# Four-layer attention and feed-forward stack on one core: first stacks over two DMA queues, three PSUM banks each for maxima and scores, values of two key tiles every four steps

## The chip, the cores and the metric

One core of one Trainium2 chip runs the whole program. The metric is the device time of one launch in microseconds. A compute engine is called PE (TensorE), DVE (VectorE), ACT (ScalarE) or POOL (GpSimd); SP is the sync engine, which here only issues DMAs.

## The reference, cut to what matters

Eight sequences of 512 rows and 256 features go through four layers. Each layer is an attention and a feed-forward part with residuals. The change touches the one program stage that computes three of these parts: the cross attention of layer 0, its "ffn" (an attention with gates), and the cross attention of layer 1.

```
q, k, v = heads(x @ Wq.T + bq), heads(ctx @ Wk.T + bk), heads(ctx @ Wv.T + bv)   # 16 heads of 16
attn = softmax(q @ k.T / sqrt(16));  out = (attn @ v) @ Wo.T + bo;  x = x + out
# gated part: q from the row's own norm, direction and temperature; k and v from x itself;
# head output times a gate from softmax(h @ Wr), softmax(h @ Ws) and the top 3
```

## The kernel before, in words

The stage is `softmax_attentions`. It works through 24 items (8 sequences of layer 0's cross attention, kind "cross"; 8 of the gated one, kind "mixture"; 8 of layer 1's cross attention), and each item has 32 steps. Every engine runs the same nest, item by item and step by step (`rounds`), from two rounds ahead of the first item (numbers -2 and -1) to one behind the last. Nothing schedules at run time: the order of each engine's instructions is what its `steps` function writes, and tables of (step, what, half) put the side work.

One step of one item does two of the 64 score tiles and two of the 64 tiles for maxima:

- **M**, `for_maximum` (L745): queries times keys into one bank of `ps_max`, 128 queries by 512 keys; DVE reduces the bank to a row maximum (`maximum`, L479). It runs `LEAD` = 12 steps ahead of the scores. There are 2 banks, so M number u waits for the reduction of M number u-2.
- **S**, `score` (L734): keys times queries, with the negated maxima as extra rows of the stacked operand, into `ps_sc`. ACT takes the exponential (`exponentials`, L661). There are 4 banks, used as two pairs: one step's two S fill a pair, and one ACTIVATE of 1024 columns empties it into `probs`, which has 4 slots (of one step each).
- **V**, `values` (L756): at every odd step, four heads' probabilities of one key tile times `vpad` (16 value columns and a column of ones, 32 columns per head), on four column tiles of PE at once, summed in `ps_out` over four key tiles. PE shows 8 matmuls for it. Every 8 steps ACT copies `ps_out` out (`take_out`, L669, step 2 of 8), and the first V of the next group of heads waits for that copy.
- **Fills** share one bank, `ps_t`, and each waits until the one before has been taken: projections "k" and "q" (L768), "v" and "y" (L776, 8 matmuls), transposes "xnT", "hT" (L763) and "raw" (L814), and "negmax" (L808), which turns the negated maxima. ACT then writes them beside the queries (`take_negmax`, L674), DVE takes v (L495), raw (L504, L506) and y (L583, or L587 in mixture items). The table `TURNS` says at which step each is made: in a cross item, for instance, v at steps 9 and 10, hT at 11 and 12, negmax at 5, 13, 21, 29.

The order of S and M on PE is S M S M at odd steps and M S S M at even ones, then V at odd steps.

Operands are stacked: the three bf16 parts of queries and keys go to a scratch in HBM (L304) and come back as 12 DMAs of 256 KB per item, 16 partitions each (`stacked`, L299), 6 for `kstack` and 6 for `qstack`. The first M of an item waits for all 12 (`stack_in`). For the first item, in the lead-in, SP issues the 6 of keys, the 6 of queries, then the second item's context (`kv_in`, L286), then six sequences of x. PE's order puts the second item's two "k" fills, which read that context, before the first M.

## Time and profile before

| what | value |
|---|---|
| median of 3 runs | 4552.01 us (4549.38 to 4552.75) |
| the profiled execution, its own time | 4549.59 us |
| its span, first to last instruction | 4547.6 us |
| PE busy, share of the span | 4283.4 us, 94% |
| DVE busy | 2994.0 us, 66% |
| ACT busy | 2515.0 us, 55% |

The span is what the profile divides; 2.0 us lie around it. Busy PE means that a matmul is under way: its end is modelled, and matmuls overlap, so 94% doesn't mean that PE could not take more. A line such as L745 is a line of the kernel before; in the changed one the numbers are some ten to twenty higher.

### The profile page before, as it was taken

The page shows a single profiled execution, that of the slowest core. Times are in us where ns is not written, and L with a number is a line of the kernel's source. Part 1 is how long each engine was busy: PE and PEld are TensorE (multiplying, and loading weights), DVE is VectorE, ACT ScalarE, POOL GpSimd, SP SyncE. Part 2 cuts the span into 40 slices and gives each one's busy share as a digit, 9 for nine tenths or more (in the row PEclk, how much of TensorE's full clock was granted, in tenths as well). Part 3 has the DMA queues.
Part 4 walks back from the last instruction along what each step waited for, and adds up shares of the span by engine and source line. Part 5 has one row for each costly group of instructions (what it writes and reads, how often), then busy time and mean ns, then how long its engine had stood idle before and what let it go on. Part 6 is the DMA issues. An engine that isn't in the chain of part 4 may idle for free. (4 is left out here: it accounts for less than half of the span.)

```text
span 4547.6 us, 65866 instructions
## 1 busy us (share of the span) xinstructions
PE 4283.4 (94%) x23716; PEld 2379.6 (52%) x23750; DVE 2994.0 (66%) x7431; ACT 2515.0 (55%) x5640; POOL 810.0 (18%) x550
## 2 busy tenths in 40 slices
PE   5999999999999998779898999999999998999999
PEld 2333343433333333458544666666666666556555
DVE  4777677777677775978685676776766666344333
ACT  2666666656566666543464767677776766111111
POOL 2323335353323220532100000000000000000000
PEclk7999999999999999899898999999999999999999
DMA  7464463535354550100101110101101001000000
GB/s 141 73 86 74 61 84 68 70 56 75 54 83 68 76 84 23 42 10 19 75 1 33 31 32 26 36 27 31 31 27 36 29 29 69 8 5 5 10 5 10
DMA packets 182839, 204.92 MB, mean 45 GB/s; under 512 B 44651, under 2 KB 165099, under 8 KB 180854
## 3 DMA queue, kind: packets, MB, share of 16 engines
q1 hardware_dynamic: 182518, 200.72, 24.2%
q8 instruction: 192, 3.15, 0.3%
q14 instruction: 129, 1.06, 0.1%
HBM read 139.90 MB, written 60.78 MB: 44 GB/s over the span
## 5 line engine op out<-in xcount | busy, mean ns | idle before, releaser
L479 DVE TENSOR_REDUCE L0x_maxes<-L0x_ps_max 128x1 f32<-128x512 f32 x1536 | 988.6, 685 | 297.4 <-PE L0x_ps_max L745 296.1
L661 ACT ACTIVATE L0x_probs<-L0x_ps_sc 128x1024 f32<-128x1024 f32 x768 | 778.0, 1026 | 421.7 <-PE L0x_ps_sc L734 416.0
L745 PE MATMUL L0x_ps_max<-L0x_kstack,L0x_qstack 96*128 96x512 bf16 x1536 | 590.7, 385 | 27.3 <-DVE L0x_maxes L479 22.6
L2736 ACT ACTIVATE L3x_pexp<-L3x_ps,L3x_nmax 128x77 f32<-128x77 f32 (+2 forms) x1536 | 601.3, 433 | 0.0
L734 PE MATMUL L0x_ps_sc<-L0x_qstack,L0x_kstack 104*128 104x512 bf16 x1536 | 523.0, 382 | 11.0 <-ACT L0x_probs L661 6.5
L2618 DVE TENSOR_REDUCE L3x_nmax<-L3x_ps 128x2 f32<-128x154 f32 (+2 forms) x768 | 346.6, 507 | 241.8 <-PE L3x_ps L2849 239.4
L756 PE MATMUL L0x_ps_out<-L0x_probs,L0x_vpad 128*32 128x512 f32 x3072 | 411.5, 608 | 9.0 <-ACT L0x_heads_raw L669 8.6
L2744 ACT COPY L3x_pT<-L3x_ps 128x512 f32<-128x512 f32 x512 | 275.1, 593 | 225.8 <-PE L3x_ps L2857 225.4
L2236 ACT ACTIVATE L3f_act_g<-L3f_ps_gu 128x512 f32<-128x512 f32 x128 | 76.4, 597 | 542.1 <-PE L3f_ps_gu L2282 542.0
L745 PEld LDWEIGHTS L0x_ps_max<-L0x_kstack,L0x_qstack 96*128 96x128 bf16 x1536 | 149.1, 97 | 418.0 <-DVE L0x_maxes L479 322.2
L2634 DVE TENSOR_SCALAR L3x_pexp<-L3x_pexp,L3x_rsum 128x77 f32<-128x77 f32 (+2 forms) x1536 | 358.1, 307 | 6.8
L2736 ACT ACTIVATION_READ_ACCUMULATOR L3x_pexp<-L3x_ps,L3x_nmax 128x1 f32 x1536 | 359.5, 235 | 0.0
L2179 DVE TENSOR_TENSOR L3f_h<-L3f_act_g,L3f_ps_gu 128x512 f32<-128x512 f32 x128 | 88.0, 688 | 382.9 <-ACT L3f_act_g L2236 382.6
L2875 PE MATMUL L3x_ps<-L3x_pT,L3x_v 128*64 128x128 f32 x4096 | 279.9, 279 | 0.7 <-ACT L3x_oT L2752 0.7
L2857 PEld LDWEIGHTS L3x_ps<-ident,L3x_pexp 128*128 128x128 f32 x2048 | 239.2, 141 | 73.5 <-issue 55.5
L2857 PE MATMUL L3x_ps<-ident,L3x_pexp 128*128 128x128 f32 x2048 | 266.1, 273 | 0.9 <-DVE L3x_pexp L2634 0.9
L2579 POOL TENSOR_TENSOR L3x_v<-L3x_v,L3x_relv 128x256 f32<-128x256 f32 x32 | 23.4, 731 | 1294.0 <-ACT L3x_v L2719 1294.0
L2282 PE MATMUL L3f_ps_gu<-L3f_xnT,L3f_wg 128*128 128x512 f32 x512 | 243.0, 597 | 1.9 <-DMA L3f_wd<-in_L3f_wd 1.9
L2293 PE MATMUL L3f_ps_y<-L3f_wd,L3f_h 128*128 128x256 f32 x1024 | 242.4, 380 | 1.5 <-DVE x_res L2189 1.5
L2875 PEld LDWEIGHTS L3x_ps<-L3x_pT,L3x_v 128*64 128x64 f32 x4096 | 218.3, 136 | 43.4 <-issue 42.4
L2282 PE MATMUL L3f_ps_gu<-L3f_xnT,L3f_wu 128*128 128x512 f32 x512 | 240.6, 592 | 0.0
L2293 PEld LDWEIGHTS L3f_ps_y<-L3f_wd,L3f_h 128*128 128x128 f32 x1024 | 193.3, 190 | 81.1 <-issue 53.8
(377 smaller groups left out, 6778.1 us busy)
## 6 DMA issues: line engine op xcount, KB each, us to landing
L0x_kstack<-parts_scratch SPq DMA_DIRECT2D x144, 256.0 KB, 10.0
L0x_qstack<-parts_scratch SPq DMA_DIRECT2D x144, 256.0 KB, 14.8
parts_scratch<-L0x_kparts SPq DMA_DIRECT2D x24, 768.0 KB, 3.7
parts_scratch<-L0x_qparts SPq DMA_DIRECT2D x24, 768.0 KB, 5.0
rel_scratch<-L3x_rel_e SPq DMA_DIRECT2D x32, 408.0 KB, 2.4
L3x_rel_d<-prob_scratch SPq DMA_DIRECT2D x32, 408.0 KB, 3.1
L0x_kv_in<-in_ctxT SPq DMA_DIRECT2D x16, 512.0 KB, 4.5
L3x_rel_t<-rel_scratch SPq DMA_DIRECT2D x32, 154.0 KB, 2.4
```

Of the source, the lines that this page charges most:

```text
L479: V.tensor_reduce(maxes[:, t, head:head + 1], ps_max[:, unit % 2, :], AX.X, ALU.max).then_inc(max_taken, 1)
L661: nc.scalar.activation(probs[:, n % 4], ps_sc[:, 2 * (n % 2):2 * (n % 2) + 2, :], ACT.Exp, scale=HD ** -0.5).then_inc(probs_ready, 1)
L734: i = nc.tensor.matmul(ps_sc[:, 2 * (n % 2) + j, :], kstack[q.parity][:, head, kt * P:(kt + 1) * P], qstack[q.parity][:, head, :], start=T ...
L745: nc.tensor.matmul(ps_max[:, unit % 2, :], qstack[q.parity][0:ROWS, head, t * P:(t + 1) * P], kstack[q.parity][0:ROWS, head, :], start=Tru ...
L756: i = nc.tensor.matmul(ps_out[32 * j:32 * j + 32, :], vpad[q.parity][:, kt, 4 * g + j, :], probs[:, (pairs + j // 2) % 4, j % 2, :], start ...
L2282: i = nc.tensor.matmul(ps_gu[:, n % 2, k], w[:, ci, n * P:(n + 1) * P], xnT[:, ci, :], start=(ci == 0), stop=(ci == C - 1))
L2293: i = nc.tensor.matmul(ps_y[:, n % 2, 0:D], h[:, e % 2, hc, t * P:(t + 1) * P], wd[:, 2 * e + hc, :], start=(hc == 0), stop=(hc == 1))
L2618: i = V.tensor_reduce(nmax[:, n % 4, s], ps[:, bank:bank + 2, a:b], AX.X, ALU.max, negate=True)
L2634: i = V.tensor_scalar(pexp[:, m % 4, e, a:b], pexp[:, m % 4, e, a:b], rsum[:, m % 4, s, e:e + 1], None, ALU.mult)
L2736: i = nc.scalar.activation(pexp[:, n % 4, e, a:b], ps[:, SB + 2 * (n % 2) + e, a:b], ACT.Exp, bias=nmax[:, n % 4, s, e:e + 1], accum_out=s ...
L2857: i = nc.tensor.transpose(ps[:, TB + e, kt * P:(kt + 1) * P], pexp[:, m % 4, e, kt * P:(kt + 1) * P], ident[:])
L2875: i = nc.tensor.matmul(ps[DIMH * e:DIMH * (e + 1), OB, at:at + P], v[g % 2][:, vt, h * DIMH:(h + 1) * DIMH], pT[:, m % 2, e, kt * P:(kt + ...
```

## The change: what it does

1. In the lead-in, ACT's queue issues the odd ones of the first item's 12 stacks, and SP's the even ones; SP issues the second item's context between its three key stacks and its three query stacks. For that the first item's values are made in the round before (`FIRST`), since the context may not be overwritten before them.
2. `ps_max` and `ps_sc` have three banks each (`BANKS`), every matmul taking the next bank. The exponential of a step is two ACTIVATEs of 512 columns, each signalled by itself.
3. V comes every fourth step (`PER`), at step 1 of 4, with the 16 matmuls of two key tiles behind one another. `probs` has 6 slots (`SLOTS`), and for the room `vpad` is packed at 17 columns per head. V at step n uses the steps n-5 to n-2 (before: n-3 and n-2).
4. The order is M S S M only at the step behind V, and S M S M at the three others.

```diff
-FIRST = [(2, "k", 0), (3, "k", 1), (14, "xnT", 0), (18, "xnT", 1), (24, "q", 0), (26, "q", 1)]
+FIRST = [(2, "k", 0), (3, "k", 1), (14, "xnT", 0), (18, "xnT", 1), (24, "q", 0), (26, "q", 1), (29, "v", 0),
+         (30, "v", 1)]
...
-        vpad = [ph.sb(f"vpad{b}", [P, TILES, HEADS, 32], F32) for b in range(2)]
+        vpad = [ph.sb(f"vpad{b}", [P, TILES, HEADS * (HD + 1) + 15], F32) for b in range(2)]
...
-        probs = ph.sb("probs", [P, 4, 2, S], F32)
+        probs = ph.sb("probs", [P, SLOTS, 2, S], F32)
...
-        ps_max = ph.ps("ps_max", [P, 2, S], F32)
-        ps_sc = ph.ps("ps_sc", [P, 4, S], F32)
+        ps_max = ph.ps("ps_max", [P, BANKS, S], F32)
+        ps_sc = ph.ps("ps_sc", [P, BANKS, S], F32)
...
-                for r, part in enumerate(part_of):
-                    sp.dma_start(stack[q.parity][HD * r:HD * r + HD, :, :],
-                                 scratch[here, part].rearrange("c (h d) s -> d (c h) s", d=HD)
-                                 ).then_inc(stack_in, 16)
+                for r in range(len(part_of)):
+                    if q.later or r % 2 == 0:
+                        stack_rows(sp, q, here, part_of, stack, r)
...
             def exponentials(q, n):
-                act.wait_ge(score_ps, q.count(STEPS, n + 1))
-                if n % 2 == 0 and (q.later or n >= 4):
-                    act.wait_ge(probs_used, q.count(STEPS // 2, n // 2 - 1))
-                nc.scalar.activation(probs[:, n % 4], ps_sc[:, 2 * (n % 2):2 * (n % 2) + 2, :], ACT.Exp,
-                                     scale=HD ** -0.5).then_inc(probs_ready, 1)
+                step = q.count(STEPS, n)
+                if step >= SLOTS and (step - SLOTS) % PER == 0:
+                    act.wait_ge(probs_used, (step - SLOTS) // PER + 1)
+                for j in range(2):
+                    at = q.count(64, 2 * n + j)
+                    act.wait_ge(score_ps, at + 1)
+                    nc.scalar.activation(probs[:, step % SLOTS, j], ps_sc[:, at % BANKS, :], ACT.Exp,
+                                         scale=HD ** -0.5).then_inc(probs_ready, 1)
...
+                if q.number == -1:
+                    for here, part_of, stack, out in ((0, k_part, kstack, k_out), (1, q_part, qstack, q_out)):
+                        act.wait_ge(out, 16)
+                        for r in range(1, len(part_of), 2):
+                            stack_rows(act, Item(0), here, part_of, stack, r)
...
-                if j == 0 and (q.later or n >= 2):
-                    pe.wait_ge(probs_ready, q.count(STEPS, n - 1))
+                at = q.count(64, 2 * n + j)
+                if at >= BANKS:
+                    pe.wait_ge(probs_ready, at - BANKS + 1)
...
-                if q.later or unit >= 2:
-                    pe.wait_ge(max_taken, q.count(64, unit - 1))
+                at = q.count(64, unit)
+                if at >= BANKS:
+                    pe.wait_ge(max_taken, at - BANKS + 1)
...
                     own = q if m < STEPS else q.plus(1)
-                    if n % 2 == 1 and q.there:
+                    behind_values = n % PER == 2
+                    if not behind_values and q.there:
                         score(q, n, 0)
                     if own.there:
                         for_maximum(own, 2 * (m % STEPS))
-                    if n % 2 == 0 and q.there:
+                    if behind_values and q.there:
                         score(q, n, 0)
...
-                    if n % 2 == 1 and (q if n > 1 else q.plus(-1)).there:
-                        values(q if n > 1 else q.plus(-1), (n - 3) % STEPS, q.there)
+                    if n % PER == 1 and (q if n > 1 else q.plus(-1)).there:
+                        values(q if n > 1 else q.plus(-1), (n - 5) % STEPS, q.there)
```

**PE, steps 11 to 13 of a cross item, before** (L763 is an hT fill, L808 negmax, L756 V, L745 M, L734 S):

```order
L763 MATMUL L0x_ps_t<-ident,L0x_htok 128x128 x4
L734 MATMUL L0x_ps_sc<-L0x_qstack,L0x_kstack 128x512
L745 MATMUL L0x_ps_max<-L0x_kstack,L0x_qstack 128x512
L734 MATMUL L0x_ps_sc<-L0x_qstack,L0x_kstack 128x512
L745 MATMUL L0x_ps_max<-L0x_kstack,L0x_qstack 128x512
L756 MATMUL L0x_ps_out<-L0x_probs,L0x_vpad 32x512 x4
L763 MATMUL L0x_ps_t<-ident,L0x_htok 128x128 x4
L745 MATMUL L0x_ps_max<-L0x_kstack,L0x_qstack 128x512
L734 MATMUL L0x_ps_sc<-L0x_qstack,L0x_kstack 128x512 x2
L745 MATMUL L0x_ps_max<-L0x_kstack,L0x_qstack 128x512
L808 MATMUL L0x_ps_t<-identb,L0x_negmax 8x128 x4
```

**The same steps now** (L782 the hT fill, L827 negmax, L760 M, L750 S):

```order
L782 MATMUL L0x_ps_t<-ident,L0x_htok 128x128 x4
L750 MATMUL L0x_ps_sc<-L0x_qstack,L0x_kstack 128x512
L760 MATMUL L0x_ps_max<-L0x_kstack,L0x_qstack 128x512
L750 MATMUL L0x_ps_sc<-L0x_qstack,L0x_kstack 128x512
L760 MATMUL L0x_ps_max<-L0x_kstack,L0x_qstack 128x512
L782 MATMUL L0x_ps_t<-ident,L0x_htok 128x128 x4
L750 MATMUL L0x_ps_sc<-L0x_qstack,L0x_kstack 128x512
L760 MATMUL L0x_ps_max<-L0x_kstack,L0x_qstack 128x512
L750 MATMUL L0x_ps_sc<-L0x_qstack,L0x_kstack 128x512
L760 MATMUL L0x_ps_max<-L0x_kstack,L0x_qstack 128x512
L827 MATMUL L0x_ps_t<-identb,L0x_negmax 8x128 x4
```

V has gone from between the two hT fills; it now stands, twice as long, only behind step 13, and step 12 has its S first.

**SP's queue in the lead-in, before:**

```order
L304 DMA parts_scratch<-L0x_kparts 128x6x512
L304 DMA parts_scratch<-L0x_qparts 128x6x512
L299 DMA L0x_kstack<-parts_scratch 16x16x512 x6
L299 DMA L0x_qstack<-parts_scratch 16x16x512 x6
L286 DMA L0x_kv_in<-in_ctxT 128x1024
L864 DMA x_res<-in_x 128x4x256 x6
```

**SP's queue there now:**

```order
L313 DMA parts_scratch<-L0x_kparts 128x6x512
L313 DMA parts_scratch<-L0x_qparts 128x6x512
L289 DMA L0x_kstack<-parts_scratch 16x16x512 x3
L296 DMA L0x_kv_in<-in_ctxT 128x1024
L289 DMA L0x_qstack<-parts_scratch 16x16x512 x3
L884 DMA x_res<-in_x 128x4x256 x6
```

**ACT there now** (L695 takes the first item's q, L701 copies the second item's xnT):

```order
L695 ACTIVATE L0x_qf<-L0x_ps_t,L0x_bqk_cross 128x512 x2
L289 DMA L0x_kstack<-parts_scratch 16x16x512 x3
L289 DMA L0x_qstack<-parts_scratch 16x16x512 x3
L701 COPY L0x_xnT<-L0x_ps_t 128x512
L284 CAST L0x_kstack<-own 8x4x128 x16
L701 COPY L0x_xnT<-L0x_ps_t 128x512
```

Six of the twelve stacks have moved to ACT, ahead of its 17 small copies, and the context has moved ahead of the query stacks. PE's fills up to the first M keep their order.

## Rows read from the trace of the kernel before

**Rows 1.** Windows (busy us of each engine): the stage, a cross item, a mixture item.

```profile
94.00:1794.00 1700.00, 1635.81 (x8583) 647.25 (x8581) 1235.91 (x2466) 1098.91 (x1148) 551.00 (x276) 0.99 0.49 69
...
302.99:372.46 69.47, 68.15 (x353) 26.21 (x352) 49.78 (x98) 46.02 (x50) 19.67 (x11) 1.00 0.53 76
882.16:959.71 77.55, 72.74 (x386) 30.96 (x385) 58.20 (x122) 46.31 (x51) 34.10 (x15) 0.98 0.44 62
```

**Rows 2.** The page's costliest groups: busy us, mean ns of one, idle before.

```profile
L479 DVE TENSOR_REDUCE L0x_maxes<-L0x_ps_max 128x1 f32<-128x512 f32 x1536 | 988.6, 685 | 297.4 <-PE L0x_ps_max L745 296.1
L661 ACT ACTIVATE L0x_probs<-L0x_ps_sc 128x1024 f32<-128x1024 f32 x768 | 778.0, 1026 | 421.7 <-PE L0x_ps_sc L734 416.0
```

**Rows 3.** Waits within 94 to 1794 us: total us, times, longest.

```profile
PEld L0x_ps_max L745 <- DVE L0x_maxes L479: 310.8, 557, 3.5
...
PEld L0x_ps_sc L734 <- ACT L0x_probs L661: 33.2, 62, 1.1
```

**Rows 4.** Timeline of PE, steps without fills: start us, us, instruction, idle before.

```profile
368.71 0.39 PE L745 MATMUL L0x_ps_max<-L0x_kstack,L0x_qstack 96*128 96x512 bf16 x1
368.93 0.38 PE L734 MATMUL L0x_ps_sc<-L0x_qstack,L0x_kstack 104*128 104x512 bf16 x1
369.36 0.39 PE L745 MATMUL L0x_ps_max<-L0x_kstack,L0x_qstack 96*128 96x512 bf16 x1
369.68 1.06 PE L756 MATMUL L0x_ps_out<-L0x_probs,L0x_vpad 128*32 128x512 f32 x8
370.67 0.39 PE L745 MATMUL L0x_ps_max<-L0x_kstack,L0x_qstack 96*128 96x512 bf16 x1
```

**Rows 5.** Timeline of DVE at the same place.

```profile
367.96 2.54 DVE L479 TENSOR_REDUCE L0x_maxes<-L0x_ps_max 128x1 f32<-128x512 f32 x4 [0.42 <-PE L0x_ps_max L745]
```

**Rows 6.** Timeline of ACT: instructions of 512 columns behind one another, and take_negmax.

```profile
320.13 0.58 ACT L669 COPY L0x_heads_raw<-L0x_ps_out 128x512 f32<-128x512 f32 x1
320.59 0.60 ACT L691 COPY L0x_hT<-L0x_ps_t 128x512 f32<-128x512 f32 x1
...
362.59 1.86 ACT L674 CAST L0x_qstack<-L0x_ps_t 8x2048 bf16<-8x2048 f32 x1
```

**Rows 7.** Timeline of PE: fills and what follows them.

```profile
316.52 1.99 PE L776 MATMUL L0x_ps_t<-L0x_wv_cross,L0x_kv_in 128*128 128x256 f32 x8
318.35 0.38 PE L745 MATMUL L0x_ps_max<-L0x_kstack,L0x_qstack 96*128 96x512 bf16 x1
...
321.81 0.66 PE L763 MATMUL L0x_ps_t<-ident,L0x_htok 128*128 128x128 f32 x4
322.31 0.38 PE L745 MATMUL L0x_ps_max<-L0x_kstack,L0x_qstack 96*128 96x512 bf16 x1
```

**Rows 8.** Timeline of the lead-in: SP's issues, ACT's small copies, PE.

```profile
32.35 4.03 SPq L299 DMA_DIRECT2D L0x_kstack<-parts_scratch  x6
36.95 7.93 SPq L299 DMA_DIRECT2D L0x_qstack<-parts_scratch  x6
...
41.96 8.38 ACT L280 CAST L0x_kstack<-own 8x512 bf16<-8x512 f32 x16
...
44.92 2.34 SPq L286 DMA_DIRECT2D L0x_kv_in<-in_ctxT  x1
...
65.60 3.75 PE L768 MATMUL L0x_ps_t<-L0x_kv_in,L0x_wk_cross 128*128 128x512 f32 x4 [22.50 <-DMA L0x_kv_in<-in_ctxT]
...
73.71 0.63 PE L745 MATMUL L0x_ps_max<-L0x_kstack,L0x_qstack 96*128 96x512 bf16 x1
```

**Rows 9.** Windows while stacks land, then while x loads: last three granted clock, DMA share, GB/s.

```profile
34.00:62.00 28.00, 5.99 (x16) 3.96 (x16) 9.86 (x22) 9.56 (x18) 3.61 (x2) 0.50 1.14 127
62.00:73.00 11.00, 6.62 (x8) 2.49 (x9) 0.00 (x0) 0.69 (x1) 0.00 (x0) 0.50 1.07 314
```

**Rows 10.** A mixture item's gate arithmetic on DVE, and PE behind it.

```profile
927.78 1.84 DVE L565 TENSOR_TENSOR L0x_gshare<-L0x_gtop,L0x_grec 128x4 f32<-128x4 f32 x1
...
933.59 0.39 PE L745 MATMUL L0x_ps_max<-L0x_kstack,L0x_qstack 96*128 96x512 bf16 x1 [2.99 <-DVE L0x_maxes L479]
```

More of the change, by code:

```diff
@@ L160, in softmax_attentions @@
     LEAD = 12
+    BANKS = 3
+    SLOTS = 6
+    PER = 4
     x_sb, ident, identb, own_rows = G["x"], G["ident"], G["identb"], G["own"]
@@ L258, in due @@
             return [(x, w, c) for x in near if x.there for m, w, c in TURNS[x.kind]
-                    if m == n and q.number + shift(w, c) == x.number]
+                    if m == n and q.number + shift(w, c) == x.number and (x.later or w != "v")]
         def occupant(q, n):
@@ L281, in own_key_rows, with stack_rows @@
             return i
+        def stack_rows(engine, q, here, part_of, stack, r):
+            engine.dma_start(stack[q.parity][HD * r:HD * r + HD, :, :],
+                             scratch[here, part_of[r]].rearrange("c (h d) s -> d (c h) s", d=HD)
+                             ).then_inc(stack_in, 16)
         @block.sync
@@ L313, in steps @@
                     if nxt.number >= 2:
-                        sp.wait_ge(score_ps, nxt.plus(-2).count(STEPS, STEPS))
+                        sp.wait_ge(score_ps, nxt.plus(-2).count(64, 64))
                     stacked(nxt, 0, k_part, kstack)
-                if q.number == -1:
-                    sp.wait_ge(q_out, nxt.count(16, 16))
-                    stacked(nxt, 1, q_part, qstack)
                 if ahead.there and ahead.cross and ahead.later:
@@ L322, in steps @@
                     context(ahead)
+                if nxt.there:
+                    sp.wait_ge(q_out, nxt.count(16, 16))
+                    stacked(nxt, 1, q_part, qstack)
                 if q.number == -1:
@@ L326, in steps @@
                     load_weights("L0f", "mixture")
-                if q.number >= 0 and nxt.there:
-                    sp.wait_ge(q_out, nxt.count(16, 16))
-                    stacked(nxt, 1, q_part, qstack)
                 if q.number == SEQS + 1:
@@ L494, in take_v @@
                 dve.wait_ge(in_bank["v"], q.count(2, half + 1))
-                V.tensor_tensor(vpad[q.parity][:, 2 * half:2 * half + 2, :, 0:HD],
+                V.tensor_tensor(vpad[q.parity][:, 2 * half:2 * half + 2, 0:HEADS * (HD + 1)]
+                                .rearrange("p b (h e) -> p b h e", h=HEADS)[:, :, :, 0:HD],
                                 ps_t[:].rearrange("p (b h d) -> p b h d", b=2, h=HEADS),
@@ L667, in take_out @@
                     act.wait_ge(in_bank["raw"], q.count(4, g - 1))
[L668 removed]
+                act.wait_ge(probs_used, q.count(STEPS // PER, 2 * g + 2))
                 nc.scalar.copy(heads_raw[:, g % 2, :], ps_out[:, :]).then_inc(out_taken, 1)
@@ L730, in score @@
                     pe.wait_ge(odd_own_ready, 1)
-                if j == 0 and (q.later or n >= 2):
-                    pe.wait_ge(probs_ready, q.count(STEPS, n - 1))
+                at = q.count(64, 2 * n + j)
+                if at >= BANKS:
+                    pe.wait_ge(probs_ready, at - BANKS + 1)
                 head = 4 * g + 2 * pair + j
-                i = nc.tensor.matmul(ps_sc[:, 2 * (n % 2) + j, :], kstack[q.parity][:, head, kt * P:(kt + 1) * P],
-                                     qstack[q.parity][:, head, :], start=True, stop=True)
-                if j == 1:
-                    i.then_inc(score_ps, 1)
+                nc.tensor.matmul(ps_sc[:, at % BANKS, :], kstack[q.parity][:, head, kt * P:(kt + 1) * P],
+                                 qstack[q.parity][:, head, :], start=True, stop=True).then_inc(score_ps, 1)
             def for_maximum(q, unit):
@@ L742, in for_maximum, with values @@
                     pe.wait_ge(stack_in, q.count(192, 192))
-                if q.later or unit >= 2:
-                    pe.wait_ge(max_taken, q.count(64, unit - 1))
-                nc.tensor.matmul(ps_max[:, unit % 2, :], qstack[q.parity][0:ROWS, head, t * P:(t + 1) * P],
+                at = q.count(64, unit)
+                if at >= BANKS:
+                    pe.wait_ge(max_taken, at - BANKS + 1)
+                nc.tensor.matmul(ps_max[:, at % BANKS, :], qstack[q.parity][0:ROWS, head, t * P:(t + 1) * P],
                                  kstack[q.parity][0:ROWS, head, :], start=True, stop=True).then_inc(max_ps, 1)
-            def values(q, pairs, waited):
-                g, kt = pairs // 8, pairs % 8 // 2
+            def values(q, first, waited):
+                g = first // 8
                 if not waited:
-                    pe.wait_ge(probs_ready, q.count(STEPS, pairs + 2))
-                if kt == 0 and (g >= 1 or q.later):
+                    pe.wait_ge(probs_ready, q.count(64, 2 * (first + PER)))
+                if first % 8 == 0 and (g >= 1 or q.later):
                     pe.wait_ge(out_taken, q.count(4, g))
-                for j in range(4):
-                    i = nc.tensor.matmul(ps_out[32 * j:32 * j + 32, :], vpad[q.parity][:, kt, 4 * g + j, :],
-                                         probs[:, (pairs + j // 2) % 4, j % 2, :], start=(kt == 0),
-                                         stop=(kt == TILES - 1), tile_position=(0, 32 * j))
+                for k in range(2):
+                    kt = first % 8 // 2 + k
+                    for j in range(4):
+                        head = 4 * g + j
+                        i = nc.tensor.matmul(ps_out[32 * j:32 * j + 32, :],
+                                             vpad[q.parity][:, kt, (HD + 1) * head:(HD + 1) * head + 32],
+                                             probs[:, q.count(STEPS, first + 2 * k + j // 2) % SLOTS, j % 2, :],
+                                             start=(kt == 0), stop=(kt == TILES - 1), tile_position=(0, 32 * j))
                 i.then_inc(probs_used, 1)
```

3 lines of the change are left out of this document (1 added, 2 removed).

## The prediction

> **What bounds the kernel now.** I read the windows first. The change touches one stage; it takes 1700 us between 94 and 1794 us, and in it PE is busy 1636 us, DVE 1236 us and ACT 1099 us [rows 1]. So PE sets the pace, but the reader is to see that a cross item of 69.5 us already has DVE at 49.8 us, and a mixture item of 77.6 us at 58.2 us: there is no room to add much to DVE. Then I took the costliest groups for the price of one reduction (685 ns) and of one exponential of 1024 columns (1026 ns) [rows 2], and the waits for who stops PE: its weight loads wait 311 us in total for the reductions, 33 us for exponentials [rows 3]. A weight load waits while the matmul before it still streams, so that sum is not lost time. What is lost shows in PE's timeline between starts. Without a wait, M and S start 0.22 us apart (368.71, 368.93), M to V takes 0.32 and V 0.99 (369.68 to 370.67) [rows 4]. The M at 369.36 comes 0.43 us behind the S at 368.93: 0.21 us are a wait for the second bank. DVE does four reductions in 2.54 us [rows 5], so one each (2.54 - 0.68) / 3 = 0.62 us when back to back, I take 0.60 to 0.62, while M and S alone would bring one each 0.44 us. DVE is behind during M and S and catches up under V and under fills. I add up a cross item's own PE work: 128 M and S at 0.22 = 28.0 (unrounded 0.219), 16 V at 1.09 = 17.4, eight fills of 1.83 us (316.52 to 318.35) = 14.6, eight transposes at 0.50 (321.81 to 322.31) = 3.9, four negmax at about 0.3 = 1.3 [rows 7]; together 65.2 us. The other 4.3 of 69.5 us are waits.
>
> **The change part by part.**
>
> *V in pairs.* Each V costs 1.09 us: 0.10 on the way in, 0.99 for itself and the way out [rows 4]. Of two behind one another one way in and one way out fall away. The way out isn't shown alone; the bounds are 0 (the next V's weights cost as much) and 0.25 us, I take 0.09, so 0.18 a pair, like the way in. 8 pairs x 24 items x 0.18 = 35 us, all PE's own work: 1.4 us an item. That is not yet a gain, since V was also DVE's and ACT's time to catch up.
>
> *Three banks and the order.* I replayed the eight groups of four steps of a cross item, from the end of one V to the end of the next, with these prices: M and S 0.22, reduction 0.69 and pace 0.60, fills as above, `take_negmax` 1.86 [rows 6], and 0.2 us from a matmul's start to its reader, 0.06 from a reader's end to the next matmul. An exponential of 512 columns isn't in the trace. The bounds are half of 1026 = 513 ns and the 0.60 us of ACT's 512-column copy; I take the copy's 0.60, as it has the same size and source. Behind one another, the copies at 320.13 and 320.59 start 0.46 us apart though the first lasts 0.58 [rows 6]; so I take a pace of 0.50 for exponentials, and keep 0.60 as the bad end. The groups come to 7.3 (steps 2 to 5), 7.9, 9.9, 10.4, 10.2, 8.2, 8.5 and 6.5 us (the last has steps 30 to 1), in sum 68.8 us against 69.5. PE's own work is then 63.8, and waits are 5.0 against 4.3. What goes: in steps without fills the third bank lets PE place the third M while the first is reduced, and a wait of about 0.5 us per four steps shrinks to 0.1 or 0.3; two waits of fills behind `take_negmax` vanish under the longer V. What comes: in steps 10 to 13 the hT fills, two normalisations and the negated maxima now all stand in one burst with no V between, and I find 1.1 us of waits there (0.5 of them negmax waiting for DVE, 0.4 an M); behind each copy of `ps_out` the exponentials are late for the third score bank, 0.1 to 0.7 us in steps 26 to 29. The first V after the copy no longer waits, but the raw fill at step 4 does, 0.3 us. Net -0.7 us an item, 14 cross items in full swing: **-10 us**. Bounds per item: -3.5 (nearly all waits go) and +2 (ACT at its bad end, below).
>
> ACT's fixed cost is where the Trainium skill speaks against the change ("ScalarE: Activation LUTs", the section on what happens when an exp ACTIVATE runs): 186 ns plus 0.833 ns per column, and neighbours overlap by about 93 ns. That makes 1039 ns for 1024 columns, and the trace agrees (1026), but it makes a pace of 519 ns for 512, slower than mine: five groups an item later by some 0.06 us, 22 items, 7 us. By the page the whole sum below would be -31 instead of -38 us.
>
> *Mixture items.* The same -0.7, and one place more: at steps 20 to 23 DVE does the gates (one tiny multiplication takes 1.84 us), and PE then waits 2.99 us for a bank for M [rows 10]. DVE stays the limit there, but with a third bank PE places one M more before it stops, and the V that now stands behind step 25, not 23, no longer keeps the y fill from starting when DVE comes back. I replay 1.5 us earlier at step 25. Eight items x 2.2 = **-18 us**; bounds 0 and -3.5 an item.
>
> *Lead-in.* PE's second-item k fills start at 65.60 when the context lands, and the first M comes at 73.71, 8.1 us later [rows 8]. The 12 stacks are 3.1 MB, and DMA moves 127 GB/s while they land against 314 GB/s for x [rows 9]: 25 us of transfer at the first rate. Now ACT can issue the odd key stacks as soon as the keys' parts are in scratch, some 4 us before SP's 32.35 us; I keep the rate of 127 GB/s, and the last stack lands near 59. The context stands behind three key stacks on SP and lands near 50. But ACT is late: it waits for the queries' parts (36.95 us before [rows 8]; 37 to 40 now, beside the early key stacks), issues three more (4.03 / 6 = 0.67 us each), copies xnT, does its small copies (8.4 us), copies xnT again: 52. Then the k fills, 3.8 us each with 0.7 us of ACT behind: first M at 62, against 73.7. I take **-11 us**. Bounds: -4 (only the early start counts) and -17 (M right behind the context's fills at 57).
>
> *At no cost:* PE's fills up to there keep their order. The packed `vpad` changes addresses, not columns. `probs` with six slots never holds ACT: the slot wanted at step n was read by the V of step n-1, which PE has issued ahead of that S. Making v early lies in PE's idle stretch before 65.6 us; without that cover it would cost two fills, 4 to 8 us.
>
> *End:* V of the last four steps is one piece, 1 us more behind the last exponential: **+1 us**.
>
> Sum: -10 - 18 - 11 + 1 = -38. The profiled execution took 4549.6 us (span 4547.6 and 2.0 around it), so 4511.6; the median of the runs lies 2.4 us above that execution, so I predict 4514 us. A measurement of this kernel can tell some 0.2%, 9 us, from no change.
>
> **The rivals.**
>
> *ACT becomes the bound (slower).* If exponentials of 512 columns follow at 0.60 us, eight of them take 4.8 us per four steps, and the 16 M and S between two V only 3.5 us. The last S needs the exponential three before it, so each group of four steps loses about 4 x (pace - 0.50): 0.4 us, 176 groups, +70 us: 4552 - 38 + 70 = 4584 us. It decides from a pace of 0.50 + 38 / (176 x 4) = 0.55 us on. For it: ACT's waits are behind PE's by little in bursts, and each exponential now signals for itself. Against it: the 0.46 us of rows 6.
>
> *Only the lead-in pays.* The longer burst costs DVE what the pair of V saves (as in steps 10 to 13), in mixture items too: 4552 - 11 = 4541 us. For it: DVE's 58.2 of 77.6 us.
>
> *The waits really go.* My replay adds every small delay in one chain; if DVE and ACT run ahead more than that, 22 items gain 3 us each: -66 - 11 = -77, 4475 us. Against it: 8 reductions at 0.60 are 4.8 us per burst of 3.5 us, whatever the banks.
>
> *It does nothing.* Context and stacks land together with ACT's late copies, and the stage is unchanged: 4552 us.
>
> **How the numbers follow.** Forecast (-20 to -60 us) 0.58; only the lead-in 0.16; waits really go 0.10; nothing 0.07; slower 0.09. The first, third and two thirds of the second lie more than 9 us below: faster 0.79. Nothing and the rest of the second: 0.12. Slower: 0.09. The range reaches from 4482 (-70 us, half of the third case) to 4550, which takes in the second case and leaves out the slower one.
>
> **What would show it.** First M (L760) near 62 us. Cross items (from one copy of `ps_out` to the same one of the next item) of 68.8 us, mixture items near 75.4; ACT's exponentials of 600 ns with starts 0.5 us apart when it lags. PE to V once per four steps, two V in about 1.9 us. The waits of L760 on DVE fewer, those of L750 on ACT more. I am wrong if L750's wait for ACT grows beyond 100 us, if steps 10 to 13 take over 10.5 us, or if the first M stays behind 70 us.

## The result, and the profile after

The changed kernel took 4504.24 us (median of 4 runs, 4500.88 to 4505.80), the kernel before beside it 4552.38 us: ratio 0.9894, 95% interval 0.9881 to 0.9906, so 48 us faster. 4514 was predicted, 4482 to 4550 as the range. The profiled execution took 4504.13 us, its span 4502.1 us.

The page's busy times and costliest groups, which answer to [rows 2], with V below:

```profile
PE 4233.5 (94%) x23716; PEld 2403.0 (53%) x23750; DVE 2976.9 (66%) x7431; ACT 2544.5 (57%) x6408; POOL 810.4 (18%) x550
...
L485 DVE TENSOR_REDUCE L0x_maxes<-L0x_ps_max 128x1 f32<-128x512 f32 x1536 | 976.5, 683 | 291.0 <-PE L0x_ps_max L760 289.3
L671 ACT ACTIVATE L0x_probs<-L0x_ps_sc 128x512 f32<-128x512 f32 x1536 | 822.7, 607 | 362.3 <-PE L0x_ps_sc L750 358.3
...
L774 PE MATMUL L0x_ps_out<-L0x_probs,L0x_vpad 128*32 128x512 f32 x3072 | 371.0, 601 | 1.1 <-ACT L0x_probs L671 1.1
```

DVE is busy 17 us less (0.6%). ACT has twice the exponentials at 607 ns and is 30 us busier, PE 50 us less.

The windows [rows 1]: a cross item, the stage, two mixture items.

```profile
278.73:346.93 68.20, 66.15 (x353) 27.07 (x352) 48.97 (x98) 47.26 (x81) 19.70 (x12) 1.00 0.54 78
94.00:1750.00 1656.00, 1576.10 (x8497) 666.61 (x8495) 1204.98 (x2434) 1115.72 (x1895) 547.46 (x272) 0.99 0.49 70
...
780.40:856.00 75.60, 70.39 (x385) 32.58 (x385) 58.10 (x122) 47.50 (x83) 34.13 (x15) 0.98 0.43 62
932.60:1007.90 75.30, 70.26 (x385) 32.27 (x385) 58.14 (x122) 47.57 (x82) 34.12 (x15) 0.98 0.45 63
```

I measure an item from its last copy of `ps_out` to the next item's. The last copy of the first item came at 164.1 us before and comes at 145.9 now (-18.2); ten cross items take 68.2 us in place of 69.5 (-12.7); the eleven intervals between them, which hold the mixture items and their side work, fell by 13.1 together; the last two (61.4 and 50.0 us, now 60.0 and 51.0) by 0.4. That is 44.4 of the 45.5 us by which the span is shorter.

Waits of PE in one cross item of the changed kernel, 282.3 to 350.5 us (total us, times, longest):

```profile
PEld L0x_ps_max L760 <- DVE L0x_maxes L485: 6.0, 9, 0.8
PEld L0x_ps_sc L750 <- ACT L0x_probs L671: 3.4, 8, 0.9
```

Before, the same two were 11.9 us in 22 waits and 1.6 in 3. In the stage the pattern is that of [rows 3] shifted: from 100 to 1740 us the loads for M wait half as long (155.9 us, 298.0 before), those for S more (74.8 us, 26.4 before).

PE's timeline in that item, the group of steps 2 to 5 and the V around it:

```profile
278.73 1.92 PE L774 MATMUL L0x_ps_out<-L0x_probs,L0x_vpad 128*32 128x512 f32 x16
...
283.00 0.63 PE L833 MATMUL L0x_ps_t<-ident,L0x_heads_raw 128*128 128x128 f32 x4 [0.45 <-ACT L0x_heads_raw L679]
...
284.66 0.39 PE L827 MATMUL L0x_ps_t<-identb,L0x_negmax 128*8 128x128 bf16 x4 [0.16 <-DVE L0x_htok L513]
...
285.64 0.38 PE L760 MATMUL L0x_ps_max<-L0x_kstack,L0x_qstack 96*128 96x512 bf16 x1
285.95 1.92 PE L774 MATMUL L0x_ps_out<-L0x_probs,L0x_vpad 128*32 128x512 f32 x16
287.81 0.39 PE L760 MATMUL L0x_ps_max<-L0x_kstack,L0x_qstack 96*128 96x512 bf16 x1
...
338.59 0.39 PE L750 MATMUL L0x_ps_sc<-L0x_qstack,L0x_kstack 104*128 104x512 bf16 x1 [0.37 <-ACT L0x_probs L671]
```

From the V's start to the next M are 1.86 us, and M to V takes 0.31 where M to S takes 0.22: a pair costs 1.86 + 0.09 = 1.95 us in place of 2 x 1.09 [rows 4], a saving of 0.23. The other two kinds of row are the waits that came: `raw` 0.45 us behind the copy, and S for an exponential.

The lead-in, against [rows 8] (SPq and ACTq are issues):

```profile
28.65 1.35 ACTq L289 DMA_DIRECT2D L0x_kstack<-parts_scratch  x3
...
33.74 2.42 SPq L289 DMA_DIRECT2D L0x_kstack<-parts_scratch  x3
...
36.71 0.36 SPq L296 DMA_DIRECT2D L0x_kv_in<-in_ctxT  x1
39.59 1.29 SPq L289 DMA_DIRECT2D L0x_qstack<-parts_scratch  x3
39.59 1.36 ACTq L289 DMA_DIRECT2D L0x_qstack<-parts_scratch  x3
...
43.09 8.39 ACT L284 CAST L0x_kstack<-own 8x512 bf16<-8x512 f32 x16
...
52.14 3.78 PE L787 MATMUL L0x_ps_t<-L0x_kv_in,L0x_wk_cross 128*128 128x512 f32 x4 [7.90 <-ACT L0x_xnT L701]
...
56.70 1.99 PE L787 MATMUL L0x_ps_t<-L0x_kv_in,L0x_wk_cross 128*128 128x512 f32 x4 [0.78 <-ACT L0x_kf L693]
...
58.52 0.81 PE L760 MATMUL L0x_ps_max<-L0x_kstack,L0x_qstack 96*128 96x512 bf16 x3
```

PE's last long wait ahead of the first M is for ACT's late copy, behind the 8.39 us of small copies. No DMA is waited for, but the margin is small: the last query stack landed at 57.5 us, 1 us ahead of the first M.

### The profile page after: what moved, and what is told of

The parts are those of the page before. It is cut to its first block and busy times, and to the rows that moved or that the text cites. A ratio compares the mean times of both kernels' runs of the same rounds, so it can differ in the third digit from the quotient of the medians.

```text
span 4502.1 us, 66443 instructions
## 1 busy us (share of the span) xinstructions
PE 4233.5 (94%) x23716; PEld 2403.0 (53%) x23750; DVE 2976.9 (66%) x7431; ACT 2544.5 (57%) x6408; POOL 810.4 (18%) x550
## 5 line engine op out<-in xcount | busy, mean ns | idle before, releaser
L485 DVE TENSOR_REDUCE L0x_maxes<-L0x_ps_max 128x1 f32<-128x512 f32 x1536 | 976.5, 683 | 291.0 <-PE L0x_ps_max L760 289.3
L671 ACT ACTIVATE L0x_probs<-L0x_ps_sc 128x512 f32<-128x512 f32 x1536 | 822.7, 607 | 362.3 <-PE L0x_ps_sc L750 358.3
L760 PE MATMUL L0x_ps_max<-L0x_kstack,L0x_qstack 96*128 96x512 bf16 x1536 | 588.0, 384 | 22.7 <-DVE L0x_maxes L485 21.3
L750 PE MATMUL L0x_ps_sc<-L0x_qstack,L0x_kstack 104*128 104x512 bf16 x1536 | 557.7, 384 | 11.5 <-ACT L0x_probs L671 11.0
L774 PE MATMUL L0x_ps_out<-L0x_probs,L0x_vpad 128*32 128x512 f32 x3072 | 371.0, 601 | 1.1 <-ACT L0x_probs L671 1.1
L760 PEld LDWEIGHTS L0x_ps_max<-L0x_kstack,L0x_qstack 96*128 96x128 bf16 x1536 | 151.0, 98 | 282.5 <-DVE L0x_maxes L485 167.5
L2877 PEld LDWEIGHTS L3x_ps<-ident,L3x_pexp 128*128 128x128 f32 x2048 | 239.1, 141 | 73.4 <-issue 55.5
L750 PEld LDWEIGHTS L0x_ps_sc<-L0x_qstack,L0x_kstack 104*128 104x128 bf16 x1536 | 150.6, 98 | 211.7 <-ACT L0x_probs L671 81.1
```

The lines of the kernel that those rows point to most:

```text
L485: V.tensor_reduce(maxes[:, t, head:head + 1], ps_max[:, q.count(64, unit) % BANKS, :], AX.X, ALU.max).then_inc(max_taken, 1)
L671: nc.scalar.activation(probs[:, step % SLOTS, j], ps_sc[:, at % BANKS, :], ACT.Exp, scale=HD ** -0.5).then_inc(probs_ready, 1)
L750: nc.tensor.matmul(ps_sc[:, at % BANKS, :], kstack[q.parity][:, head, kt * P:(kt + 1) * P], qstack[q.parity][:, head, :], start=True, stop ...
L760: nc.tensor.matmul(ps_max[:, at % BANKS, :], qstack[q.parity][0:ROWS, head, t * P:(t + 1) * P], kstack[q.parity][0:ROWS, head, :], start=T ...
L774: i = nc.tensor.matmul(ps_out[32 * j:32 * j + 32, :], vpad[q.parity][:, kt, (HD + 1) * head:(HD + 1) * head + 32], probs[:, q.count(STEPS, ...
L2877: i = nc.tensor.transpose(ps[:, TB + e, kt * P:(kt + 1) * P], pexp[:, m % 4, e, kt * P:(kt + 1) * P], ident[:])
```

## The experiments

All ratios are against the kernel before, run beside each. "Rest" is the time from the first item's last copy of `ps_out` to the last item's, in the profiled execution: it leaves the lead-in out, whose length differs by some us between kernels that share it.

| run | median us (range, runs) | ratio [95%] | cross item | first M | rest |
|---|---|---|---|---|---|
| before | 4552.38 (4549.38 to 4553.79, 4) | | 69.5 | 73.7 | 1630.4 |
| changed | 4504.24 (4500.88 to 4505.80, 4) | 0.9894 [0.9881, 0.9906] | 68.2 | 58.5 | 1604.2 |
| e1_leadin | 4538.79 (4532.22 to 4541.01, 6) | 0.9970 [0.9958, 0.9981] | 69.5 | 60.6 | 1636.7 |
| e2_order_only | 4548.47 (4545.14 to 4551.68, 10) | 0.9990 [0.9981, 1.0000] | 69.5 | 69.2 | 1630.4 |
| e8_no_leadin | 4521.82 (4518.39 to 4523.05, 4) | 0.9932 [0.9917, 0.9946] | 68.2 | 77.4 | 1604.2 |
| e3_banks_v2 | 4545.60 (4538.70 to 4551.41, 10) | 0.9987 [0.9977, 0.9996] | 69.7 | 73.4 | 1624.8 |
| e4_v4_oldbanks | 4580.81 (4576.06 to 4583.69, 4) | 1.0067 [1.0051, 1.0084] | 70.7 | 78.3 | 1654.2 |
| e5_order_before | 4508.54 (4507.08 to 4510.21, 4) | 0.9909 [0.9894, 0.9923] | 68.2 | 62.1 | 1604.6 |
| e6_max2_score4 | 4567.50 (4565.35 to 4568.60, 4) | 1.0038 [1.0023, 1.0053] | 70.7 | 61.7 | 1657.7 |
| e7_max4_score2 | 4533.00 (4529.41 to 4533.66, 4) | 0.9961 [0.9946, 0.9976] | 69.8 | 60.4 | 1635.1 |
| e9_own_on_dve | 4501.15 (4498.41 to 4505.68, 4) | 0.9880 [0.9866, 0.9893] | 68.2 | 59.8 | 1604.1 |
| e10_raw_later | 4507.98 (4507.27 to 4508.67, 4) | 0.9893 [0.9878, 0.9909] | 68.5 | 60.4 | 1611.0 |
| e11_hT_later | 4522.15 (4521.72 to 4522.42, 5) | 0.9925 [0.9912, 0.9937] | 69.5 | 60.2 | 1621.0 |
| e12_one_queue_early | 4505.97 (4504.05 to 4506.67, 4) | 0.9901 [0.9885, 0.9918] | 68.2 | 61.1 | 1603.8 |

### Which half of the change pays

**e1_leadin**: the kernel before with part 1 of the change alone.

> The kernel before with the lead-in part of the change alone (six stacks issued by ACT, context ahead of the query stacks, first values a round earlier). Theory A (the lead-in is a separate gain): the first M starts near 58.5 us as in the changed kernel instead of 73.7, and the time falls by 15 us, some 18 at most. Rival B (part of the 18 us that the first item gained comes from the third bank for maxima): first M at 58.5, but the copy that ends the first item only 13 to 15 us earlier than 164.1, so the time falls by 13 to 15 us and no more.

**e8_no_leadin**: the changed kernel with part 1 undone.

> The changed kernel with its lead-in part undone; three banks each, V in pairs and the new order stay. Theory A (the parts add up): 4552 - 48 + 15 = 4519 us, cross items 68.2 us, first M at 73.7. Rival B (the lead-in also changes the later items' phase): items other than 68.2 us and a time off that sum by over 5 us.

Part 1 alone brings 13 us, the rest alone 30, in sum 43 where both together bring 48. e1 shows where it is short. Its first M comes 2.1 us behind the changed kernel's though the code up to there is the same: its second k fill took 3.69 us, not 1.99, at a granted clock of 0.51 from 54.6 to 60.6 us. And it lost 6.2 us again in the rest: its five full mixture items take 77.5 to 78.6 us, 390.7 together against 384.4 before, with the same code. That is PE's clock. The second of these items before, PE's timeline and the window behind it:

```profile
857.69 0.39 PE L745 MATMUL L0x_ps_max<-L0x_kstack,L0x_qstack 96*128 96x512 bf16 x1 [2.99 <-DVE L0x_maxes L479]
...
857.70:864.50 6.80, 6.63 (x35) 3.11 (x39) 4.49 (x10) 2.56 (x3) 6.57 (x5) 1.00 0.23 77
```

The same item in e1, and the stretch behind the gates of the next one (last three: granted clock, DMA share, GB/s):

```profile
843.98 0.39 PE L753 MATMUL L0x_ps_max<-L0x_kstack,L0x_qstack 96*128 96x512 bf16 x1 [2.99 <-DVE L0x_maxes L482]
...
844.00:850.80 6.80, 6.63 (x25) 3.44 (x26) 2.88 (x6) 1.61 (x2) 6.57 (x5) 0.75 0.22 75
921.50:928.30 6.80, 6.78 (x21) 3.15 (x22) 2.01 (x4) 1.02 (x1) 6.57 (x5) 0.55 0.22 75
```

The stall is the same 2.99 us, but in e1 a stretch at half the granted clock follows it in all five items, in three of them twice as long; before, in three of the five, none of them long.

For e1 rival B came out: the copy that ends the first item comes 13.8 us earlier and the time falls by 13, though the first M is at 60.6 and not 58.5 us. For e8 it is theory A: 3 us above its 4519, with the changed kernel's items.

### Banks against pairs of V

**e3_banks_v2**: part 1 undone, three banks each and exponentials of 512, but V at every odd step.

```diff
-    SLOTS = 6
-    PER = 4
+    SLOTS = 4
+    PER = 2
...
-                for k in range(2):
+                for k in range(1):
```

> Lead-in as before; three banks each and exponentials of 512 columns as changed, but V every two steps with 8 matmuls and the order before (S M S M at odd, M S S M at even steps). Theory A (V in pairs frees PE time and the banks only pay for it): without pairs PE has 1.8 us an item more work; the waits for maxima shrink from about 2.5 to under 1 us an item, so a cross item takes 68 to 69.2 us and the time is 10 to 25 us below before. Rival B (the third bank alone is nearly the whole steady gain): cross item at 68.2 or less, time 30 us below before. Rival C (splitting the exponentials costs as much as the third bank gives): cross item 69.5 or more, time unchanged or longer.

**e4_v4_oldbanks**: part 1 undone, V in pairs, but the banks and exponentials of before.

```diff
-        ps_max = ph.ps("ps_max", [P, BANKS, S], F32)
-        ps_sc = ph.ps("ps_sc", [P, BANKS, S], F32)
+        ps_max = ph.ps("ps_max", [P, 2, S], F32)
+        ps_sc = ph.ps("ps_sc", [P, 4, S], F32)
```

> Lead-in as before; V in pairs every four steps, six slots and the new order as changed, but two banks for maxima and two pairs for scores with one exponential of 1024 columns a step. Theory A (V in pairs alone takes away DVE's time to catch up, and needs the third bank): bursts of eight maxima on two banks wait more than before, a cross item takes 69.5 to 71 us against 69.5 before and 68.2 changed; time 0 to +30 us against before. Rival B (the saved PE time of 0.23 us a pair is the gain whatever the banks): cross item 67.7 to 68.5 us, time 25 to 40 us below before.

Neither half gives the gain. Banks alone leave a cross item as it was (69.7 us, rival C), pairs alone make it 1.2 us longer (theory A). The 6 us in e3's median lie in the mixture items: the five full ones take 376.5 us for 384.4, an estimated 3.2 of it two half-clock stretches fewer. PE's waits for its two readers in one cross item of e3 (299.6 to 369.2 us):

```profile
PEld L0x_ps_sc L742 <- ACT L0x_probs L668: 5.4, 9, 1.1
PEld L0x_ps_max L752 <- DVE L0x_maxes L482: 5.0, 6, 0.8
```

and those of e4 for the reductions, from 100 to 1740 us:

```profile
PEld L0x_ps_max L750 <- DVE L0x_maxes L482: 303.3, 618, 3.4
```

In e3, with a third bank for maxima, M's waits are 6.9 us less, and with three banks and exponentials of 512 for scores, those of S are 3.8 more. In e4 M waits as of old, in a burst twice as long.

**e5_order_before**: the changed kernel with M S S M at every even step.

```diff
-                    behind_values = n % PER == 2
+                    behind_values = n % 2 == 0
```

> The changed kernel with the order of S and M on PE as before (M S S M at every even step, not only behind V). Theory A (order matters little, since M comes once in 0.44 us either way): cross item 68.1 to 68.5 us, time within 5 us of 4504. Rival B (alternation evens out what DVE and ACT get, and is part of the gain): cross item 68.7 us or more, time 12 us or more above 4504.

From the second item on all are the same to 0.1 us: part 4 of the change does nothing there. The 4 us in the medians lie ahead of it: the first M comes 3.5 us later, and the first item takes 2.1 us more at a granted clock of 0.90, against 0.94.

**e6_max2_score4** and **e7_max4_score2**: the changed kernel with the six banks split 2 and 4, and 4 and 2, each matmul still taking the next bank.

```diff
-        ps_max = ph.ps("ps_max", [P, BANKS, S], F32)
-        ps_sc = ph.ps("ps_sc", [P, BANKS, S], F32)
+        ps_max = ph.ps("ps_max", [P, 4, S], F32)
+        ps_sc = ph.ps("ps_sc", [P, 2, S], F32)
```

> The changed kernel with two banks for maxima and four for scores, one exponential of 512 columns per bank. Theory A (the third bank for maxima pays for V in pairs, a fourth for scores does little): waits of M on DVE grow to 4 us an item or more, cross item 69.5 to 71 us, time 4535 to 4565. Rival B (scores are the tighter side since ACT waits rose): cross item under 68.2 us, time under 4504.

> The changed kernel with four banks for maxima and two for scores. Theory A (three and three is the balance; ACT is one exponential behind at every copy and every k or q fill): S waits for ACT by 0.3 us and more in most groups of four steps, cross item 70 us or more, time 4545 or more. Rival B (DVE is the tight side and takes any bank): cross item under 68.2 us, time under 4504.

Same bursts, same instructions; only the split differs, and both sides of 3 and 3 are worse: 2.5 us per cross item with two for maxima (e4's 70.7 again, so the length of the exponential makes no difference there), 1.6 us with two for scores. In e6 the time, 4567.5, is just over the 4565 named; in e7 both figures are under what was named (70 us, 4545 us), though on the side forecast. The waits of PE from 100 to 1740 us, of e6:

```profile
PEld L0x_ps_max L760 <- DVE L0x_maxes L485: 312.2, 618, 3.5
```

and of e7:

```profile
PEld L0x_ps_sc L750 <- ACT L0x_probs L671: 260.1, 606, 0.9
...
PEld L0x_ps_max L760 <- DVE L0x_maxes L485: 63.7, 76, 0.8
```

A fourth bank for maxima does take M's waits down (63.7 us from 155.9), and ACT's take their place.

### What the lead-in waits for

**e2_order_only**: the kernel before with the context ahead of the query stacks and v early, all on SP.

```diff
-                if q.number == -1:
-                    sp.wait_ge(q_out, nxt.count(16, 16))
-                    stacked(nxt, 1, q_part, qstack)
...
+                if nxt.there:
+                    sp.wait_ge(q_out, nxt.count(16, 16))
+                    stacked(nxt, 1, q_part, qstack)
```

> As the lead-in part, but all twelve first stacks stay on SP's queue; only the context goes ahead of the query stacks and the first values are made a round earlier. Theory A (the gain is the two k fills that no longer stand behind the last transfer, 8.1 us, and the queue order does it): first M at 63 to 66 us, time -8 to -10 us. Rival B (two queues carry the stacks faster or earlier, and that is most of it): first M at 66 or later, time -5 us or less.

**e12_one_queue_early**: the changed kernel with all twelve stacks on SP, the six of keys issued as soon as the keys' parts are out, ahead of the queries' parts.

```diff
+                if q.number == -1:
+                    sp.wait_ge(k_out, 16)
+                    stacked(nxt, 0, k_part, kstack)
...
-                if q.number == -1:
-                    for here, part_of, stack, out in ((0, k_part, kstack, k_out), (1, q_part, qstack, q_out)):
-                        act.wait_ge(out, 16)
```

> The changed kernel with all twelve first stacks on SP's queue, but the six key stacks issued as soon as the keys' parts are in scratch, near 28.5 us, ahead of the queries' parts. Theory A (the second queue brings no transfer rate for stacks, only the early start of three of them, while the DMA engines would idle): six start early instead, the queries' parts then wait behind them until about 45 us, and the last stack lands at 60 to 64 us: first M there, against 58.5 to 62 with two queues and 69.2 with one queue and the late start; time 4504 to 4510 us. Rival B (two queues move stacks faster side by side): the last stack lands at 66 us or later, time 4512 or more.

**e9_own_on_dve**: the changed kernel with the second item's 16 small key copies on DVE.

```diff
+                        own_key_rows(V.tensor_copy, kstack[1]).then_inc(odd_own_ready, 1)
...
-                        own_key_rows(nc.scalar.copy, kstack[1]).then_inc(odd_own_ready, 1)
```

> The changed kernel with the 16 small copies of the odd key stack on DVE, behind the even ones, and off ACT. They stood on ACT between the two xnT copies and held the second item's k fills until 52.1 us. Theory A (the lead-in is now bound by ACT's copies, the stacks land earlier than the fills end): the k fills start at 46 to 50 us with the landing of the context, and the first M comes at 57, when DVE is done with its 15.4 us of copies or the stacks have landed, 2 to 4 us before the changed kernel's 58.5 to 62; time 0 to -4 us against 4504. Rival B (the transfers end at 58 anyway and bind): first M at 58 or later, waiting for a stack, time unchanged.

The window of 28 to 34 us (last three: granted clock, DMA share, GB/s), in the changed kernel:

```profile
28.00:34.00 6.00, 2.64 (x11) 1.48 (x9) 4.44 (x5) 0.69 (x1) 0.00 (x0) 1.00 0.82 95
```

The same window in e2, in which nothing moves yet:

```profile
28.00:34.00 6.00, 2.64 (x11) 1.63 (x10) 4.44 (x5) 0.69 (x1) 0.00 (x0) 1.00 0.00 0
```

And in e12, with the key stacks issued early in the one queue:

```profile
28.00:34.00 6.00, 3.42 (x14) 2.71 (x15) 4.33 (x5) 0.00 (x0) 0.00 (x0) 0.97 1.07 123
```

PE's timeline, what the first M waits for in e2:

```profile
69.23 1.03 PE L743 MATMUL L0x_ps_max<-L0x_kstack,L0x_qstack 96*128 96x512 bf16 x2 [6.00 <-DMA L0x_qstack<-parts_scratch]
```

And in e9:

```profile
59.78 0.82 PE L758 MATMUL L0x_ps_max<-L0x_kstack,L0x_qstack 96*128 96x512 bf16 x3 [2.29 <-DMA L0x_qstack<-parts_scratch]
```

The order alone brings the first M 4.5 us earlier and the median 3.2 us down, at the edge of its interval: PE's fills start earlier, and then the last query stack is late (rival B). The second queue adds two things. One is the stretch of 28 to 34 us, in which DMA moved nothing in e2. The other shows when both queues have stacks, from 50 to 56 us in the changed kernel:

```profile
50.00:56.00 6.00, 3.78 (x4) 1.18 (x4) 0.00 (x0) 2.10 (x5) 0.00 (x0) 0.50 1.13 198
```

The query stacks of e12, in one queue, in the same window:

```profile
50.00:56.00 6.00, 3.86 (x5) 1.26 (x5) 0.00 (x0) 1.97 (x4) 0.00 (x0) 0.50 1.15 117
```

And those of e2, from 58 to 64 us:

```profile
58.00:64.00 6.00, 4.45 (x8) 1.27 (x6) 0.00 (x0) 1.37 (x2) 0.00 (x0) 0.82 1.16 112
```

The changed kernel's six query stacks land 1.3 us apart (50.9 to 57.5 us), those of e12 2.2 us apart (50.1 to 61.1). e1 and e9, also with two queues, show 197 and 195 GB/s. So two queues did carry stacks side by side faster, 198 GB/s against 112 to 117. The Trainium skill says otherwise ("DMA: Bandwidth & Descriptors", the section on issuing engines not being separate DMA queues): all issuers share the same 16 engines, and a second one saves issue time only. For these stacks of 16 partitions the measurement decides against it; why one queue alone doesn't reach that rate was not tried. Of the 11.7 us by which the last stack lands earlier than in e2 (57.5 and 69.2 us), an estimated 6 x (2.2 - 1.3) = 5 are rate, the rest early start.

e12's time and first M fell where theory A had put them, but its premise, that the second queue brings no rate, did not hold. e12 moves six stacks early, not three, and its last one still lands at 61.1 us, so its first M waits for it (3.00 us of its load). It comes 2.6 us behind the changed kernel's, within the 58.5 to 62.1 us of kernels that share the changed lead-in; its rest is the changed kernel's. It also pays for six key stacks ahead of the queries' parts in one queue:

```profile
parts_scratch<-L0x_qparts SPq DMA_DIRECT2D x1, 768.0 KB, 13.2
```

Those land 13.2 us after their issue, against 6.2 in the changed kernel and 5.0 with nothing ahead of them (before and e2), so the query stacks are issued at 45.09 and not 39.59 us.

In e9 the first bound is gone and the next one shows: the first M waits 2.29 us for the last query stack (rival B). Its median is 3 us lower, but its before beside it was 4 us higher than the changed kernel's, and the ranges overlap; I do not count it as a gain.

### Moving the fills that wait

**e10_raw_later** and **e11_hT_later**: in the changed kernel's table of a cross item, `raw` 3 at step 6 in place of 4, and the second hT at step 14 in place of 12.

```diff
-    "cross": [(4, "raw", 3), (5, "negmax", 1), (9, "v", 0), (10, "v", 1), (11, "hT", 0), (12, "hT", 1),
+    "cross": [(5, "negmax", 1), (6, "raw", 3), (9, "v", 0), (10, "v", 1), (11, "hT", 0), (12, "hT", 1),
```

> The changed kernel with the raw fill of the last four heads at step 6 instead of 4 in cross items; it waited at step 4 for ACT's copy of ps_out of step 2. Theory A (the waits of the group of steps 2 to 5 are delays in this chain): raw no longer waits for the copy and negmax at step 5 no longer for DVE's two instructions on raw, so that group takes 0.4 to 0.8 us less, the next one 0 to 0.2 us more, a cross item 67.6 to 68.0 us, time 5 to 10 us below the changed kernel. Rival B (DVE's or ACT's pace binds the group, not the fill): cross item 68.2 us as before the edit.

> The changed kernel with the second hT fill at step 14, behind V and ahead of xnT, instead of step 12 in cross items. Steps 10 to 13 take 9.7 us there, with waits that I put to ACT's copy of the first hT, to negmax waiting for DVE, and to M. Theory A (the missing V between the two hT fills is what these steps lose): steps 10 to 13 lose 0.5 us of fill and 0.2 to 0.5 us of waits, steps 14 to 17 gain the fill and up to 0.6 us of waiting for ACT's copy, a cross item 67.9 to 68.3 us. Rival B (the wait only moves): cross item 68.3 us or more.

In e10 the group of steps 2 to 5 falls by 0.53 us (V at 280.86 and 287.55 us) and the next rises by 0.83. In e11 steps 10 to 13 stay at 9.67 us though a fill has left them, and steps 14 to 17 take 1.33 us more. PE's timeline of e11 there: hT and xnT now stand behind one another on the one bank.

```profile
309.01 0.66 PE L782 MATMUL L0x_ps_t<-ident,L0x_htok 128*128 128x128 f32 x4
310.34 0.66 PE L782 MATMUL L0x_ps_t<-ident,L0x_xn 128*128 128x128 f32 x4 [0.68 <-ACT L0x_hT L701]
```

That pair makes 0.68 of the 1.33 us, so e11 tells less than was wanted of it. I had expected gains in both. The cross item of e10 is 68.5 us, longer than either side had it; that of e11, 69.5 us, is rival B's.

## Why the prediction was right or wrong

The time lies in the range, and the working held for V and for the cross items. Two terms were wrong in size, the mixture items and the lead-in.

**V in pairs, 0.18 us a pair**: 0.23, 1.8 us an item and not 1.4.

**Waits of a cross item, 5.0 us against 4.3**: PE's own work is 65.2 - 1.8 = 63.4 us, so 4.8 us of 68.2 are waits. That was the working's central claim and it held: the whole gain of a cross item is PE's own work, and the waits are a little longer. The windows say the same without a subtraction of prices: PE is busy 66.15 of 68.20 us, before 68.15 of 69.47 [rows 1], so 2.0 us less busy and 0.7 us more idle. By the same subtraction e4 and e6 have 7.3 us of waits and e3 4.5. So three and three banks don't remove waits as a whole; they let the burst be doubled without adding 2.5 us of them. The eight groups, V to V, predicted 7.3, 7.9, 9.9, 10.4, 10.2, 8.2, 8.5 and 6.5, took 7.2, 7.9, 9.7, 10.4, 10.0, 8.1, 8.5 and 6.4 us. (The predicted ones add up to 68.9, not 68.8.) The item came to 68.2 and not 68.8: 0.4 from the pairs, 0.2 from waits. The term was -10 us for 14 items; ten full ones brought 12.7.

**Exponentials, 600 ns with a pace of 0.50**: 607 ns, and ten in a row in 5.35 us, so (5.35 - 0.60) / 9 = 0.53 us in the longest row; pairs last 1.09 us (0.49). The rival in which ACT becomes the bound, at 0.55 us, was near. The pace of 519 ns, an estimate from the Trainium skill ("ScalarE: Activation LUTs"; the figures stand in the section on what ACT_TABLE_LOAD costs, not in the one that the prediction names), lies between the two; the group of steps 30 to 1 came no later for it.

ACT's timeline, the longest row of exponentials in the item:

```profile
341.91 5.35 ACT L671 ACTIVATE L0x_probs<-L0x_ps_sc 128x512 f32<-128x512 f32 x10
```

S's waits for ACT grew to 74.8 us, under the 100 that I had named.

**Mixture items, -2.2 us each, -18**: wrong in size. The eleven intervals brought 13.1 us, the five full mixture items together 5.9 (384.4 to 378.5), 1.2 each. At the gates PE's idle time fell from 2.99 [rows 10] to 2.55 us, in all five. Behind it three of them had a stretch at half the granted clock before, and all five have now, one of them (at 907 us) twice as long. The first as a window (granted clock 0.50):

```profile
756.10:759.40 3.30, 3.30 (x10) 2.40 (x9) 1.35 (x3) 0.00 (x0) 3.22 (x3) 0.50 0.33 111
```

Before, the items with such a stretch took 77.5 us and the two without 75.9, so it costs 1.6 us; twice as long it cost 1.1 more (78.6 against 77.5 in e1). Two stretches more and one twice as long are an estimated 2 x 1.6 + 1.1 = 4.3 us of loss: without them the five would have gained 10.2, 2.0 each. By that estimate the replay of steps was nearly right, and what the term left out is PE's clock behind the stall. That the change brings these stretches is not shown. All seven kernels with V in pairs and 3 and 3 banks show it in the same five items, one of them twice as long; but with the stage of before, two (before and e2) show three and e1 shows five, three of them twice as long, behind the same stall. A fourth stretch of the kernel before, at 1293 us, is gone in the changed one. What decides is open.

**Lead-in, -11**: -18.2 to the first item's last copy, of which 15.2 are the first M, 58.5 us for 73.7. The mechanism was right (ACT's small copies last, then two k fills): the first fill came at 52.14, predicted 52; the context landed at 48.7, predicted 50; the last stack at 57.5, predicted 59, and two queues at 198 GB/s, where 127 was kept, are why it bound nothing. Three steps make the difference of 7.2. The sum was put together wrong (2.6 of it): fills from 52 and the 8.1 us of [rows 8] make 60.1, not 62, and -13.6, not -11. Then the second fill was priced at 3.8 us, its time at half clock (1.6 of the difference); it took 1.99, with a granted clock of 0.94 from 56.0 to 58.5 us. In e1 it took 3.69 and the first M came at 60.6, close to the 60.1. Last, the first item itself is 3.0 us shorter (87.4 us from first M to last copy, 90.4 before), which I had not priced. It is the third bank: at the same mean granted clock of 0.94 the first item takes 90.4 and 89.7 us with two for maxima (before, e1), and 87.4, 86.9 and 87.5 with three (changed, e3, e8). The clock counts too: 93.1 us in e4 (0.92) and 95.2 in e6 (0.89), both with two, and 89.5 in e5 (0.90) with three.

**End, +1**: the last item took 51.0 us for 50.0.

**The rivals**: "only the lead-in pays" is out by e8, "the waits really go" by the 4.8 us, "nothing" by both. The total missed by 9.8 us: +4.9 on the mixture items, -2.7 on the cross ones, -7.2 on the lead-in, -1.4 on the last two items, -1.1 behind the stage, and -2.3 because the profiled execution lies at the median here and lay 2.4 us below it before. That it came so near is in part luck: two terms were off by more than a quarter, to opposite sides.
